# The attention loop of a macaron block: the Q product of the next step moved between two products of the MLP, and one gate moved ahead of a multiplication

## The reference

```
qkv = shift(x) @ wqkv;  q, k, v = split(qkv)        # 8 heads of 64
q, k = l2norm(q) * qs, l2norm(k) * ksc
q, k = q * cos * scale + rotate_half(q) * sin * scale, (the same for k, with 1 / scale)
o = softmax(mask(8 * q @ k.T)) @ v                  # windows of 64, each sees itself and the one before
x = x + o @ wo
h = layernorm(shift(x)) @ w1 + b1;  a, g = split(h) # 341 columns each
x = x + (a * gelu(g)) @ w2 + b2
```

## Time and profile before

| | us |
|---|---|
| median of the runs | 1160.47 |
| the runs | 1160.47, 1161.17, 1155.60 |
| span of the profiled execution, first to last instruction | 1152.9 |
| PE busy in the span | 995.2 (86%) |
| DVE busy | 719.8 (62%) |
| ACT busy | 681.6 (59%) |
| POOL busy | 514.8 (45%) |

### The profile page before, as it was taken

How to read it: one execution, slowest core, us unless ns; L and a number is a source line. 1 busy time by engine, 2 the same in 40 slices (tenths; PEclk the granted TensorE clock), 3 DMA queues, 4 the chain that set the end, 5 groups by cost and what they waited for, 6 DMA issues and landing times.

```text
span 1152.9 us, 26028 instructions
## 1 busy us (share of the span) xinstructions
PE 995.2 (86%) x9072; PEld 628.5 (55%) x9072; DVE 719.8 (62%) x1657; ACT 681.6 (59%) x1311; POOL 514.8 (45%) x392
## 2 busy tenths in 40 slices
PE   4789999999998877789999999999829986856995
PEld 1445555555555347255555555556418983535995
DVE  1568677778777554477777777778674432665442
ACT  3566686686684572666676676674616654633662
POOL 2455456456442524455553453452463550363552
PEclk9989999999999987899999999999958997776998
DMA  5665454354434600444443443443422222012224
GB/s 177 159 154 135 123 146 112 91 131 112 93 94 99 78 1 3 92 112 112 111 106 86 106 111 85 102 111 75 150 89 61 67 71 74 18 49 63 61 67 128
DMA packets 89711, 109.99 MB, mean 95 GB/s; under 512 B 20368, under 2 KB 74384, under 8 KB 88816
## 3 DMA queue, kind: packets, MB, share of 16 engines
q1 hardware_dynamic: 82160, 91.17, 33.5%
q0 software_dynamic: 4544, 9.35, 2.3%
q10 hardware_dynamic: 2880, 7.81, 2.2%
HBM read 62.66 MB, written 12.07 MB: 65 GB/s over the span
## 4 chain that ended last, share of the span: by engine, by line
PE 66%; ACT 15%; issue 7%; DVE 6%; DMA 3%; POOL 2%; SPq 1%; ACTq 0%; DVEq 0%; POOLq 0%
PE banks L589 7%; PE banks L936 6%; PE banks L946 6%; PE banks L662 5%; PE banks L676 5%; PE banks L620 4%; PE banks L751 3%; PE banks L669 3%; PE banks L637 3%; PE banks L726 2%; PE banks L721 2%; PE banks L645 2%; ACT arena L1184 2%; ACT arena L1189 2%; PE banks L971 1%
## 5 line engine op out<-in xcount | busy, mean ns | idle before, releaser
L2062 POOL TENSOR_TENSOR arena<-arena 128x1024 f32<-128x1024 f32 x64 | 150.9, 2358 | 323.7 <-DVE arena L1662 317.4
L2051 POOL TENSOR_TENSOR arena<-arena 128x1024 f32<-128x1024 f32 x64 | 150.9, 2357 | 40.8 <-ACT arena L1184 40.8
L1654 DVE TENSOR_REDUCE arena<-banks 128x4 f32<-128x512 f32 x128 | 82.4, 685 | 95.1 <-PE banks L620 95.0
L1176 ACT ACTIVATE arena<-banks,arena 128x512 f32<-128x512 f32 x128 | 80.5, 679 | 92.0 <-PE banks L669 91.5
L589 PE MATMUL banks<-arena 128*128 128x512 f32 x256 | 127.2, 621 | 6.7 <-DVE arena L1554 5.9
L2041 POOL DMA_INDIRECT moe_outs<-arena x78 | 81.2, 1040 | 98.2 <-DVE arena L1904 94.1
L1397 ACT ACTIVATE arena<-banks,arena 128x128 f32<-128x128 f32 x312 | 89.0, 369 | 55.8 <-PE banks L936 55.5
L2034 POOL DMA_INDIRECT moe_rows<-arena x64 | 63.9, 998 | 94.6 <-DVE arena L1635 70.3
L1662 DVE TENSOR_TENSOR arena<-arena 128x1024 f32<-128x1024 f32 x64 | 78.0, 1219 | 24.6 <-DMA arena<-arena 24.6
L1189 ACT ACTIVATE arena<-banks 128x1024 f32<-128x1024 f32 x64 | 65.6, 1025 | 44.8 <-PE banks L589 43.9
L946 PE MATMUL banks<-arena 128*128 x624 | 86.7, 282 | 3.5 <-ACT arena L1397 2.9
(11 more groups left out here) (220 smaller groups left out, 1914.5 us busy)
## 6 DMA issues: line engine op xcount, KB each, us to landing
arena<-arena SPq DMA_DIRECT2D x256, 128.0 KB, 3.9
arena<-rstd SPq DMA_DIRECT2D x128, 256.0 KB, 4.2
arena<-moe_rows SPq DMA_DIRECT2D x78, 64.5 KB
arena<-in_mw SPq DMA_DIRECT2D x2, 2048.0 KB, 11.5
arena<-moe_outs SPq DMA_DIRECT2D x16, 256.0 KB, 4.8
arena<-in_rot ACTq DMA_DIRECT2D x12, 256.0 KB, 3.2
arena<-in_wa ACTq DMA_DIRECT2D x2, 1026.0 KB, 6.7
arena<-ssm_a SPq DMA_DIRECT2D x4, 512.0 KB, 6.6
```

What stands on the lines that cost most here:

```text
L1654: nc.vector.tensor_reduce(mx[:, e], by_row(bank[3 + e][:]), AX.X, ALU.max).then_inc(s_max, 1)
L2051: nc.gpsimd.tensor_tensor(TA[:, n % 2], RAW, ROTV[:, :, 0, c * C:(c + 1) * C], ALU.mult).then_inc(cos_done, 1)
L2062: nc.gpsimd.tensor_tensor(TA[:, n % 2], TA[:, n % 2], TB, ALU.add).then_inc(rot_sum, 1)
```

## The change

On PE, `project` is split: it now issues one product, Q (k = 0) or K (k = 1), with the waits in front of Q. In the steps with `hidden`, the Q product of the next step is issued between block 0 and block 1 of `hidden`; the next step (hp = 2) then issues K alone. Everywhere else Q and K follow each other as before. On DVE, in hp = 2, gate 2 is moved ahead of `rotate`. No instruction is added or removed.

```diff
-                def project(s, n):
-                    hp, c, d = s % HP, s // HP % NCH, s // (HP * NCH)
...
+                def project(s, k):
+
+                    if s >= STEPS:
+                        return
+                    n, hp, c, d = STEPS * run + s, s % HP, s // HP % NCH, s // (HP * NCH)
+                    if k == 0:
+                        if d == 0:
+                            need(pe, ln_out, norm0 + c + 1)
+                        else:
+                            pe.wait_ge(mlp_out, 2 * NCH * run + c + 1)
+                        if run == 0 and s % (HP * NCH) == 0:
+                            pe.wait_ge(wa_in[d], 16)
+                        after(pe, copied, 2 * n)
+                    w0 = k * INNER + hp * P
+                    mm(bank[k], w_qkv[d][:, w0:w0 + P], (YA, YM)[d][:, c * C:(c + 1) * C],
+                       start=True, stop=True).then_inc(proj, 1)
...
                 for s in range(STEPS + 1):
                     n, hp, g = STEPS * run + s, s % HP, s // HP
-                    if s < STEPS:
-                        project(s, n)
-                    elif run:
+                    if hp != 2 or g < 2:
+                        project(s, 0)
+                    project(s, 1)
+                    if s == STEPS and run:
...
                     if hp == 1 and g >= 2:
-                        for j in range(3):
-                            hidden(g - 2, s, j)
+                        hidden(g - 2, s, 0)
+                        project(s + 1, 0)
+                        hidden(g - 2, s, 1)
+                        hidden(g - 2, s, 2)
...
                     if s >= 2:
                         normalise(s - 2, n - 2)
+                    if hp == 2 and g >= 2:
+                        gate(g - 2, gg - 2, 2)
                     if s >= 1:
                         rotate(s - 1, n - 1)
-                    if hp == 2 and g >= 2:
-                        gate(g - 2, gg - 2, 2)
```

## The result

The changed kernel takes 1148.16 us (median of 15 runs, 1145.94 to 1152.18), the kernel before 1156.67 us (15 runs, 1152.39 to 1161.17). The ratio is 0.9936, with a 95% interval of 0.9921 to 0.9952: 0.64% faster, some 7.4 us (5.6 to 9.1), where 1.2 us and "no change" were forecast. Of the 11.1 us between the forecast 1159.3 and the measured time, 3.8 us are chance: the three runs shown before the prediction had a median of 1160.47, the fifteen have 1156.67.

What follows compares the result with a forecast made beforehand. F looked bound by PE, but ACT was taken to end the step behind `hidden`. Site terms 1.1 + 0.41 + 0.17 - 0.24 - 0.32 gave 1.2 us saved: 1160.47 - 1.2 = 1159.3 us, 8-in-10 range 1154.0 to 1163.0.

Steps and rivals of the forecast that it cites:

- PE leaves this step when ACT lets it: Step behind `hidden`: ACT, not PE's own products, ends it; ACT waited only 0.51 us before the squares in step 10.
- I count nothing: Gate 2 ahead of the sine product on DVE: up to 0.4 us on PE, all within PE's waiting for ACT.
- The other 0.35 to 0.65 us that PE has won goes into waiting for ACT's squares and V copies: Step behind `hidden`, second F: of PE's gain only 0.19 us shortens the step; the rest becomes waiting.
- its own sign: Second F, distance between such steps, 42.85 us: shrinking by over 0.5 us would mean ACT wasn't the limit.
- the term for the Q product: Q moved into the slot between blocks 0 and 1 of `hidden`: 1.2 us saved over both loops.
- the delay of the blocks: Blocks 1 and 2 of `hidden` behind Q: 0.32 us late at seven sites, about 0.08 at five.
- the second and third blocks then come 0.32 us late at seven sites: `hidden`, six sites of second F and step 9 of first: 0.21 us overlap plus 0.11 for a late-starting product.
- 0.51 - 0.32: ACT's idle before the squares less the blocks' delay: squares and V copies 0.19 us earlier per second F site.
- The first F was right in kind: First F, site by site: 0.41 us saved at step 30, 0.17 at step 18; 0.24 lost at three, 0.32 at step 10.
- Rival 1: Whole of Q is won at all twelve sites: 0.86 us each, 10.3 us, giving 1150.1 us; chance 0.10.
- 0.11 for faster by over 0.5%: Whole kernel: chance of a gain beyond 0.5% (5.8 us), from rival 1 and a lucky median.
- a largest saving of 3.7 us: Forecast's upper bound, both loops: no delay of the blocks at all, 6 x 0.5 + 0.49 + 0.25 us.

Runs made afterwards that it cites:

- the carry late: Kernel before, with the carry of V moved behind the second copy of V: ratio 1.0013 (0.9993 to 1.0034), 42.91 us a group in the second F.
- Q alone: Changed kernel with gate 2 back behind the sine product: ratio 0.9984 (0.9968 to 0.9999), 42.53 us a group in the second F.
- all late: Changed kernel with the small Exp between the third and fourth copy of V and the carry behind the second: ratio 0.9970 (0.9951 to 0.9989).

## Why the prediction was wrong

The step that failed is the reading of who ends the step behind `hidden`: "PE leaves this step when ACT lets it", and from it "I count nothing" for gate 2 and "The other 0.35 to 0.65 us that PE has won goes into waiting for ACT's squares and V copies". The runs showed that PE's own products up to the first V product ended that step before the change (the carry late won nothing), and that gate 2 was worth 3.2 of the 5.8 us (Q alone won 2.6). The prediction named its own sign for this: a distance that shrinks by over 0.5 us means that ACT wasn't the limit; it shrank by 0.62. Besides, the term for the Q product was too small, 1.2 us where Q alone won 2.6; the delay of the blocks in it was put at 0.32 us and measured 0.10. For one site of the second F, from the scores of the step with `hidden` (547.11 before, 544.24 after) to the event, against the rows above:

| event | forecast | measured |
|---|---|---|
| start of block 1's gate product | +0.32 | 3.67 - 3.46 = +0.21 |
| start of GELU 2 | +0.32 | 6.59 - 6.50 = +0.09 |
| start of the Exp | +0.32 | 8.59 - 8.49 = +0.10 |
| start of the squares | -0.19 | 9.75 - 10.27 = -0.52 |
| first copy of V | -0.19 | 14.01 - 14.64 = -0.63 |
| next transposes | -0.19 | 16.48 - 17.11 = -0.63 |

- "the second and third blocks then come 0.32 us late at seven sites": 0.10. Block 1 did start 0.21 us later; the 0.11 us that the prediction added came from a misread row. The 0.97 us between block 1's two products were not a late start of the linear one behind its wait: the gate product itself takes longer when its weights are loaded only as it starts, 0.70 us for its first instruction in place of 0.59. Weight loads of block 1's gate product, before (the load begins with the product, at 550.57):

```profile
550.57 0.30 PEld L721 LDWEIGHTS banks<-arena 128*128 128x128 f32 x2 [1.32 <-ACT arena L1210]
```

  and after, where it lies under the Q product, 0.2 us ahead of block 1 at 547.91:

```profile
547.70 0.39 PEld L724 LDWEIGHTS banks<-arena 128*128 128x128 f32 x2 [0.47 <-ACT arena L1216]
```

  So block 1 follows Q with no gap (0.11 us less than reckoned), and its two products are 548.77 - 547.91 = 0.86 us apart in place of 0.97 (another 0.11). Term: 0.22 us a site. By the rule that the prediction weighed (the Trainium skill, TensorE: Matmul & The Clock Gate, "Step-by-step: what each phase is for") weights are pulled ahead of running matmuls; here the trace agrees.
- The squares were put 0.19 us earlier, "0.51 - 0.32". They came 0.52 earlier: 0.22 by the point above, and 0.11 because, once they no longer wait for PE, they start while the second Exp is still listed (553.99 against 552.83 + 1.27). By the Trainium skill (ScalarE: Activation LUTs, "What ACT_TABLE_LOAD costs") back-to-back ACTIVATEs overlap by about 93 ns; the trace comes near it with 0.11 us.
- "PE leaves this step when ACT lets it": not so before the change. The first copy of V began 0.14 us behind the carry with no idle listed; it waited for PE's product, as the run with the carry late shows. After the change the copy follows the carry within 0.03 us (558.25 against 557.58 + 0.64), so ACT could come earlier by another 0.11 us: 0.19 + 0.22 + 0.11 + 0.11 = 0.63. It also means that PE's gain behind the squares was no spare time. PE and ACT together give the step: PE's first V product starts 0.78 us earlier with gate 2 ahead (556.88 - 544.24 = 12.64 for 13.42) and 0.33 with Q alone, ACT allows 0.63, and the later of the two decides: 0.63 with the gate, 0.32 without.
- Gate 2, "I count nothing": 0.30 us a site in the second F, 3.2 us over all twelve, more than half of what was won. The prediction had the wait (transposes at about 556.5, gate 2 at about 556.7) and wrote it off as time in which PE waits for ACT anyway. Its bound, up to 0.4 us, held.
- The first F was right in kind (least at step 10, most at step 30, ACT late where the small Exp stands) and 0.3 to 0.4 us a site too low throughout. Gate 2 accounts for 0.2 to 0.4 us of that (Q alone against changed, group by group), except at the first site, where the two groups are equal, 42.81 us; the rest isn't separated there.
- Rival 1, the whole 0.86 us, was nearer in time (1150.1 us), but partly by the 3.8 us of the starting point: of its 10.3 us, 5.8 lie in the loops. Of 0.86 us a site in the second F, 0.78 us reach the output transposes (553.47 - 544.24 = 9.23 for 557.12 - 547.11 = 10.01) and 0.63 the end of the step: 0.08 went to the blocks and 0.15 was lost at ACT's carry, which now stands right ahead of the first copy of V. Moving the carry gave 0.09 of that back (42.14 us, all late).
- The chances: 0.11 for faster by over 0.5% rested on a largest saving of 3.7 us, which counted listed idle alone and no gain from the gate.

## What to carry to other kernels

The views here list no idle under 0.15 us (the 0.14 us ahead of the first copy of V isn't listed), so two engines that hand over with "no idle" may be nearly tied; before you name one of them the master, compare the start with the end of what it needs on both sides. Two edits of one change are not to be priced apart: a wait that is covered by what the first edit takes away becomes the next limit, and the second edit is worth just what the first lays bare. When an engine's idle time is to be filled, look for the slot by its releaser: the same product, with gate 2 ahead, was worth 0.62 us a group of the second F in a slot that ended with ACT's GELU and nothing one block later.

## What was unexpected of the hardware

A 128x512 float32 product whose weights are loaded only as it starts is listed with 0.70 us for its first instruction, one whose weights were loaded earlier with 0.59 (0.43 to the next start): filling an idle slot shortens the product behind it by 0.11 us as well. A wait on PE isn't needed for it: a step's first gate product stands behind the scores with no idle listed and has 0.70 us too.

```profile
590.95 0.70 PE L721 MATMUL banks<-arena 128*128 128x512 f32 x1
```

In the whole trace of the kernel before, the median is 0.70 us for the 144 such instructions whose weights are loaded as they start, 60 of them behind a listed idle, and 0.59 us for the other 752. Marks inside a loop repeat to 0.02 us from one execution to another (42.23 us in ten groups of two profiles), except in the first F's first group (42.81 and 42.97 us), while the stages behind the second F differ by up to 10 us in executions of kernels that don't differ there.
